# Query norms in a stage of their own, query products spread over the slots, outputs as triples: one change to a Perceiver layer on one core

## The reference

```
x = layernorm(x)
q = rmsnorm(x @ Wq, gq)                 # per head of 128 columns
k = rmsnorm(ctx @ Wk, gk);  v = ctx @ Wv
scores = q @ k.T / sqrt(128)            # 32 x 257 for each batch and head
out = softmax(scores) @ v
x1 = x + out @ Wo
```

## Time and profile before

| | |
|---|---|
| median of 3 runs | 2919.72 us (2918.31 to 2921.80) |
| profiled execution, own time | 2916.03 us |
| its span | 2914.2 us |
| mean granted TensorE clock | 0.944 |
| busy: PE, DVE, ACT, POOL | 2624.2, 2102.3, 1753.7, 1110.5 us |
| stages: keys; weights; attention's main block; the rest | to 770; 770 to 815; 815 to 2166; to 2914 us |

### The profile page before, as it was taken

One profiled execution on the slowest core, in us unless ns is written; L12 is line 12 of the kernel. 1 busy time (PEld: TensorE's weight loads), 2 busy tenths in 40 slices (PEclk: granted clock), 3 DMA queues, 4 the chain that ended last, 5 costly groups with the idle time before them and its releaser, 6 DMA issues. The chain is left out here.

```text
span 2914.2 us, 51949 instructions
## 1 busy us (share of the span) xinstructions
PE 2624.2 (90%) x14275; PEld 2095.6 (72%) x14275; DVE 2102.3 (72%) x4976; ACT 1753.7 (60%) x3450; POOL 1110.5 (38%) x1357
## 2 busy tenths in 40 slices
PE   8999999999779999999999999999968778847998
PEld 6777777777657888888888888888853434335887
DVE  7999999999556667766666677766644666667886
ACT  6777777777545566655556666655652433315776
POOL 0100010011024444544444444544425565634775
PEclk9999999999889999999999999999987878767999
DMA  1000000100222222222222222222220001020111
GB/s 45 25 24 24 24 24 26 31 24 25 91 58 67 65 84 84 82 65 73 69 68 72 73 84 84 73 70 68 69 71 22 22 22 44 15 80 30 55 51 39
DMA packets 191005, 154.56 MB, mean 53 GB/s; under 512 B 20658, under 2 KB 186899, under 8 KB 190227
## 3 DMA queue, kind: packets, MB, share of 16 engines
q1 hardware_dynamic: 190866, 153.14, 18.5%
HBM read 138.38 MB, written 14.69 MB: 53 GB/s over the span
## 5 line engine op out<-in xcount | busy, mean ns | idle before, releaser
L251 DVE TENSOR_REDUCE kn_ssq<-kn_sq 128x8 f32<-128x1024 f32 x514 | 620.6, 1215 | 71.7 <-ACT kn_sq L193 65.3
L193 ACT ACTIVATE kn_sq<-kn_keys 128x1024 f32<-128x1024 f32 x514 | 527.9, 1027 | 177.1 <-PE kn_keys L142 174.6
L748 ACT ACTIVATE ca_sc<-ca_sc,ca_low 128x257 f32<-128x257 f32 x512 | 254.4, 499 | 251.5 <-DVE ca_low L868 251.5
L930 POOL TENSOR_TENSOR ca_sc<-ca_sc,ca_rden 128x1028 f32<-128x1028 f32 x128 | 243.3, 1901 | 407.1 <-DVE ca_rden L850 407.1
L142 PE MATMUL kn_keys<-kn_wk_hi,kn_ct_hi 128*128 128x512 f32 x1028 | 334.5, 406 | 1.0 <-ACT kn_sq L193 1.0
L142 PE MATMUL kn_keys<-kn_wk_lo,kn_ct_hi 128*128 128x512 f32 x1028 | 319.9, 392 | 0.0
L142 PE MATMUL kn_keys<-kn_wk_hi,kn_ct_lo 128*128 128x512 f32 x1028 | 319.7, 392 | 0.0
L676 PE MATMUL ca_b_out<-ca_vo,ca_oT 128*128 128x256 f32 x1024 | 245.9, 383 | 2.9 <-ACT ca_oT L756 0.7
L823 DVE CUSTOM_DVE_ANT_0 ca_sc<-ca_b_sc,ca_rk,ca_rq_rows 128x257 f32<-128x257 f32 x512 | 229.9, 482 | 5.4 <-PE ca_b_last L657 3.7
L142 PEld LDWEIGHTS kn_keys<-kn_wk_lo,kn_ct_hi 128*128 128x128 f32 x1028 | 193.3, 188 | 44.5
L142 PEld LDWEIGHTS kn_keys<-kn_wk_hi,kn_ct_lo 128*128 128x128 f32 x1028 | 193.2, 188 | 43.4
(11 more groups left out here) (281 smaller groups left out, 6640.4 us busy)
## 6 DMA issues: line engine op xcount, KB each, us to landing
ca_rk<-key_norms SPq DMA_DIRECT2D x512, 128.5 KB, 2.9
kn_rows<-in_ctx_dram SPq DMA_DIRECT2D x128, 128.0 KB, 2.4
ca_rows<-in_ctx_dram SPq DMA_DIRECT2D x128, 128.0 KB
ca_xin<-in_x_dram SPq DMA_DIRECT2D x32, 128.0 KB, 2.7
ca_xres<-in_x_dram SPq DMA_DIRECT2D x32, 128.0 KB, 3.1
x_after_attention<-ca_x SPq DMA_DIRECT2D x32, 128.0 KB, 2.8
tm_xg<-x_after_attention SPq DMA_DIRECT2D x8, 512.0 KB, 4.6
tm_xr<-x_after_attention SPq DMA_DIRECT2D x8, 512.0 KB, 4.9
```

The costliest lines, as they stand in the source:

```text
L193: act.activation(sq[c][:, :], keys[c][:, :], ACT.Square).then_inc(sq_ready, 1)
L251: dve.tensor_reduce(ssq[s][:, t * H + c * (H // 2):t * H + (c + 1) * (H // 2)], sq[c][:, :].rearrange("p (h d) -> p h d", d=P), AX.X, ALU. ...
L748: act.activation(sc[n][:, g, :], sc[n][:, g, :], ACT.Exp, bias=low[n][:, g:g + 1], scale=1.0, accum_out=den[n][:, g:g + 1]).then_inc(exp_r ...
L930: pool.tensor_tensor(sc[m][:, :, :], sc[m][:, :, :], rden[m][:, :].unsqueeze(2).broadcast_to((P, 4, SKV)), ALU.mult)\
```

## The change

1. A new stage `query_norms` between `key_norms` and `cross_attention` normalises x, computes x Wq for all 32 tiles of 128 queries, and stores the transposed normalised x in parts (`xT`, 512 KB a superblock) and the inverse query norms (`rq`) in HBM. Wq is loaded and split by POOL during `key_norms`.
2. In `cross_attention` the phase of query products is gone. The first superblock's pairs of heads are made up front; those of the next superblock are made in the slots of the present one: none in slot 0, one in slots 1 to 6, two in slot 7. They use the bank `b_cols`, which `turn_ctx` uses too.
3. Outputs are triples: `oT` and `vo` are split (new DVE work `out_lo`).
4. The 257th key leaves `values`: its softmax weights are collected for four batches in 4 rows of `b_last`, stored, reloaded as a block-diagonal matrix and multiplied with the last keys' output rows (`last_values`, made up front), two matmuls a quad into `b_out`. The one-column casts go to POOL (`last_key`).
5. The program's loop is two superblocks long.

The core of the diff of `cross_attention`:

```diff
+        def pairs_ahead(b, bb):
+            if isinstance(b, int) and not 0 <= b < B - PER:
+                return ()
+            n = bb % PER
+            return (n - 1, n) if n == PER - 1 else (n - 1,) if n else ()
+        def pairs_before(b, bb):
+            n = b + PER - (bb % PER != 0)
+            return min(n, B) if isinstance(b, int) else n
...
         @block.tensor
...
+            def queries_ahead(b, bb, r, n):
...
+                pe.wait_ge(clo_ready, b + 2)
+                if n == PER - 1:
+                    pe.wait_ge(ulo_ready, b + PER)
+                queries(b_cols, n, xT[odd], odd)
             def turn_ctx(b, bb):
...
                 ge(pe, clo_ready, b)
+                ge(pe, ulo_ready, pairs_before(b - 1, bb - 1) if not isinstance(b, int) or b > 0 else 0)
...
-                    mm = pe.matmul(b_out[:, 0:DIM], oT[n][:, h, :], vo[:, h, :], start=(h == 0), stop=(h == H - 1))
+                    triple(b_out[:, 0:DIM], (oT_hi[n][:, h, :], oT_lo[n][:, h, :]), (vo_hi[:, h, :], vo_lo[:, h, :]), h == 0, False)
...
                 if live(b):
+                    scores(b, bb, 2)
+                    scores(b, bb, 3)
+                ahead = pairs_ahead(b, bb)
+                if ahead:
+                    queries_ahead(b, bb, r, ahead[0])
                 if live(b - 2):
                     values(b - 2, bb - 2)
+                if ahead[1:]:
+                    queries_ahead(b, bb, r, ahead[1])
...
         @block.scalar
...
                         act.activation(sc[n][:, g, :], sc[n][:, g, :], ACT.Exp, bias=low[n][:, g:g + 1], scale=1.0,
                                        accum_out=den[n][:, g:g + 1]).then_inc(exp_ready, 1)
+                ahead = pairs_ahead(b, bb)
+                if ahead:
+                    act.wait_ge(sc_ready, 4 * b + 4)
+                    queries(b_cols, 1 - bb // PER, ahead[0], b + PER)
                 if live(b - 2):
...
+                    act.activation(oT_hi[q][:, :, c * SQ:(c + 1) * SQ], b_val[:, :].rearrange("p (h q) -> p h q", q=SQ), ACT.Copy)\
+                        .then_inc(ohi_ready, 1)
+                if ahead[1:]:
+                    queries(b_cols, 1 - bb // PER, ahead[1], b + PER + 1)
...
         @block.vector
...
+            def slot(b, bb, r):
+                if live(b - 3):
+                    out_lo(b - 3, bb - 3, r)
...
                     dve.tensor_scalar(low[bb % 2][:, :], top[bb % 2][:, :], -1.0, None, ALU.mult).then_inc(low_ready, 1)
-                    split_last(b, bb)
...
+                for k, n in enumerate(pairs_ahead(b, bb)):
+                    queries(b_cols, 1 - bb // PER, n, b + PER + k)
...
         @block.sync
...
+                if bb % 4 == 2 and live(quad(bb, r) - 1, QUADS):
+                    Q = quad(bb, r) - 1
+                    n = (bb // 4 + 1) % 2
+                    store_stray(Q, n)
...
+                if bb % 4 == 3 and live(quad(bb, r) - 1, QUADS):
+                    load_stray(quad(bb, r) - 1, (bb // 4 + 1) % 2, 32 * (2 * r + (bb // 4 - 1) // 2 + 1))
```

More of the change, by code:

```diff
@@ L578, in triple, with queries @@
                 return pe.matmul(out, a_lo, w_hi, start=False, stop=final)
[L580 to L583 removed]
+            def queries(bank, n, x, odd):
+                for k in range(2):
+                    h = 2 * n + k
                     for a in range(2):
[L585 to L586 removed]
@@ L682, in slot @@
+                    pe.matmul(b_out[:, 0:DIM], ps_diag[n][:, :], vs_rows[n][:, 0, :], start=False, stop=False)
+                    pe.matmul(b_out[:, 0:DIM], ps_diag[n][0:64, :], vs_rows[n][0:64, 1, :], start=False, stop=True).then_inc(out_ready, 1)
+            def slot(b, bb, r):
+                Q = quad(bb - 6, r)
+                turn_p.r = r
                 if live(b + 1):
-                    turn_ctx.i = i
                     turn_ctx(b + 1, bb + 1)
                 if live(b - 2):
-                    turn_p(b - 2, bb - 2, i)
+                    turn_p(b - 2, bb - 2)
@@ L754, in slot @@
                     if c == 0:
-                        ge(act, out_ready, (b - 2) // 4 - 1 if isinstance(b, int) else 2 * i + (bb - 2) // 4 - 1)
-                    act.activation(oT[q][:, :, c * SQ:(c + 1) * SQ], b_val[:, :].rearrange("p (h q) -> p h q", q=SQ), ACT.Copy)\
-                        .then_inc(oT_ready, 1)
-            def body(i):
-                queries(i)
-                for bb in range(PER):
-                    slot(PER * i + bb, bb, i)
+                        ge(act, out_ready, quad(bb - 2, r) - 1)
@@ L808, in ctx_lo, with queries @@
+            def queries(bank, odd, n, done):
+                dve.wait_ge(uhi_ready, done)
+                dve.tensor_tensor(u_pair(u_lo, odd, n), bank[:, :].rearrange("p (h b q) -> p h b q", h=2, b=PER), u_pair(u_hi, odd, n).bitcast(F32),
+                                  ALU.subtract).then_inc(ulo_ready, 1)
             def ctx_lo(b, bb):
@@ L931, in slot @@
                         .then_inc(norm_ready, 1)
+                if live(b + 1):
+                    last_key(b + 1, bb + 1)
                 if live(b):
                     split_rows(b, bb)
-                if bb == 4 and i is not None and (not isinstance(i, int) or i + 1 < SBS):
-                    inverse_std(i + 1)
-            def body(i):
-                query_norms(i)
-                for bb in range(PER):
-                    slot(PER * i + bb, bb, i)
-            pool.wait_ge(const_ready, 8)
-            inverse_std(0)
-            run(pool, body, slot)
+            pool.wait_ge(stray_split, 2)
+            pool.wait_ge(const_ready, 4)
+            last_key(0, 0)
+            run(pool, slot)
 def time_mixing(nc, held, x1_dram, mu_dram, wx1_dram, wx2_dram, wr_dram, ww1_dram, ww2_dram, bw_dram, wk_dram, wv_dram,
```

652 lines of the change are left out of this document (367 added, 285 removed).

## The result

The changed kernel takes 3007.78 us (median of four runs, 3006.28 to 3009.52), the kernel before 2919.01 beside it: a ratio of 1.0304, interval 1.0286 to 1.0322. It is slower, as forecast, but by 89 us and not by 155; the time lies under the range's low end of 3020. The profiled execution has a span of 3007.7 us, 93.5 more than before.

What follows compares the result with a forecast made beforehand. Attention was taken as bound by the VectorE and ScalarE chain, with TensorE the limit in query products; 250 - 7.3 + 0 + 2 - 105 + 6 + 9 = +155; forecast 3074 us, range 3020 to 3140.

Steps and rivals of the forecast that it cites:

- break-even: Attention slots: the changed kernel is faster once a slot with a pair is under 7.8 us; forecast slot 9.28.
- the superblocks' term, -105: Attention loop: a superblock takes 75.5 us against 82.5, so 105 us less over 15.
- `turn_ctx` to `scaled` 2.59 less 0.31 = 2.28: End of a slot with a pair: 2.28 us from `turn_ctx` to the next `scaled`, three narrow transposes (0.31) gone.
- reciprocal to `scaled` 0.41: Slot without a pair: 0.41 us from VectorE's reciprocal to `scaled`, part of its 7.3 us.
- 0.84 leaves DVE's chain: Attention slots: the 257th key's `pl` and two casts leave VectorE's chain, 0.84 us, so `low` starts 3.43 after `scaled`.
- The clock: +9 forecast: Attention slots: TensorE's idle time lowers its clock in six slots, +9 us; bounds 0 and one for each of 105 slots.
- the rival of a fall in every slot: Attention slots: the clock falls in each slot with a pair, 99 more falls at 1.5 us, 3220; chance 7%.
- The new stage: +250: `query_norms`: a loop through POOL's power sets 7.2 us a tile over PE's 5.85, +250 us; bounds 208 and 265.
- POOL hides: New stage: POOL's power does not pace it (cheaper, or ACT's squares get ahead), 42 us less, 3032; chance 12%.
- The sum of the head: Head of attention: query load, eight pairs and last keys' products take 38.9 us instead of 36.9, +2.
- DVE and ACT alone pace them: Attention slots: PE's transposes are early, slots take 8.2 us, 113 less, 2961; chance 5%.
- PE's work paces: Attention slots: `u_lo` does not hold `turn_ctx`, slots take PE's 7.68 us, 208 less, 2866; chance 8%.

Runs made afterwards that it cites:

- Experiment 1: Changed kernel with the query pairs behind the values and in the banks of the scores instead of `b_cols`: 2848.72 us, ratio 0.9766.
- experiment 2: Changed kernel with TensorE doing the values before the first query pair, same bank and same wait: 3008.25 us, ratio 1.0310.
- experiment 4: Changed kernel with outputs as plain fp32 products again, without `out_lo`: 3010.53 us, ratio 1.0311.
- Experiment 8: One more VectorE instruction per slot on the changed kernel: 3078.88 us; attention loop written out on the changed kernel: 2983.41 us, on the kernel before: 2905.94 us.
- Experiment 3: Changed kernel with GpSimd's inverse root taken one tile later in the new stage: 2976.41 us, ratio 1.0195.
- experiment 9, first run: Changed kernel with pairs in the banks of the scores, inverse roots one tile later and plain fp32 outputs: 2804.71 us, ratio 0.9618.
- second run: Changed kernel with pairs in the scores' banks, inverse roots one tile later, plain fp32 outputs and the attention loop written out: 2792.43 us, ratio 0.9571.

## Why the prediction came out as it did

*Direction: right, and shown.* The new stage costs more than the superblocks give back, and the pair in a shared bank is why they give so little. Experiment 1 takes away only that wait (experiment 2 excludes the order) and the kernel crosses to the other side. The prediction's break-even was a slot of 7.8 us; at 7.40 the kernel is faster than the one before, at 8.9 slower.

*The step that failed: the superblocks' term, -105, measured -141.* By its own parts: a slot without a pair was 6.80 and not 7.3; six with one summed to 53.7 (1308.17 to 1361.90) and not 55.7; the one with two was 12.1 (1437.31 to 1449.44) and not 12.5. That is 2.9 us a superblock, 43 in fifteen; the stops at the loop's end gave 10 of it back. The mechanism was right; three pieces of the chain were mis-sized. For a slot with one pair the first and the third below, 0.19 and 0.13, make the difference: 9.28 - 0.32 = 8.96, and 53.7 / 6 = 8.96 (single slots took 8.84 to 9.18). In all three, an end of the interval had been set by something other than what would set it in the new chain. For the first two, PE's rows of the slot before and of the slot after:

```profile
1109.55 0.40 PE L669 MATMUL ca_b_val<-ca_pl,ca_last 65*128 65x512 f32 x1
...
1109.79 0.38 PE L629 MATMUL ca_b_cols<-ca_ident,ca_rows 128*128 128x128 f32 x2
...
1111.56 0.28 PE L578 MATMUL ca_b_sc<-ca_cT_hi,ca_u_lo 128*128 128x258 f32 x1
```

```profile
1332.95 0.44 PE L850 MATMUL ca_b_cols<-ca_ident,ca_rows 128*128 128x128 f32 x2 [1.27 <-DVE ca_u_lo L1000]
...
1334.45 0.28 PE L825 MATMUL ca_b_sc<-ca_cT_hi,ca_u_lo 128*128 128x258 f32 x1
```

- "`turn_ctx` to `scaled` 2.59 less 0.31 = 2.28" began at the start of a weight load (1109.56) that lay 0.23 us ahead of its matmul (1109.79), because PE was still at the last value product. Behind an idle PE load and matmul start together (1332.95), and the interval is 2.09 (to 1335.04). The other end hid nothing: the last product of score group 0 starts 0.59 ahead of `scaled` in both slots.
- "reciprocal to `scaled` 0.41", taken for the slots without a pair, was most likely a wait for PE as well: in that slot of before `scaled` came 0.59 behind the last product of its score group, just as in the slot after, where DVE's wait ends with PE's scores. With PE early, `scaled` follows by 0.09 behind `oT_lo` and the reciprocal (2188.71 to 2188.80), and by 0.18 in experiment 4, where the reciprocal comes out of an idle stretch. Other slots of before had 0.34; what sets those was not taken apart.
- "0.84 leaves DVE's chain" counted from the start of `pl`; with the gap ahead of it 0.97 left (`low` at +4.27 before, +3.30 after). Experiment 8 puts a like instruction back at 0.56.

Only the third was sized by a run; the first two are read from the traces.

*The clock: +9 forecast, some 2 us found.* I had taken the falls of the first superblock for six more slots. Busy time by stretch in the changed kernel's first superblock, then over one of its later slots with a pair and behind the first jump at the loop's end:

```profile
1091.00:1097.00 6.00, 3.55 (x18) 3.25 (x18) 3.02 (x16) 3.12 (x12) 3.98 (x7) 0.67 0.84 222
1097.00:1103.00 6.00, 5.48 (x23) 4.88 (x23) 2.51 (x11) 1.47 (x3) 3.97 (x7) 0.50 0.25 57
1103.00:1106.00 3.00, 2.73 (x13) 2.73 (x14) 1.21 (x8) 1.72 (x7) 0.00 (x0) 0.50 0.22 65
```

```profile
1317.11:1326.11 9.00, 7.27 (x55) 6.44 (x54) 4.95 (x21) 4.30 (x14) 4.21 (x8) 1.00 0.29 83
1374.00:1376.00 2.00, 2.00 (x12) 1.92 (x11) 0.77 (x2) 1.01 (x2) 0.72 (x1) 0.50 0.45 131
```

The clock fell during the first of these stretches, in which PE was busy 3.55 of six microseconds, and stayed at 1.2 GHz (0.50) until about 1107. The first three slots took 9.08, 9.01 and 9.20 us and the fourth 8.74, so the fall cost about 1 us at most. (By reciprocals the second slot looks 3.4 us too long, 12.12, but 3.5 of it is the wait for PE ahead of its `scaled`, and the interval ahead of it is 5.73. In the kernel before, too, the reciprocals that I took the earlier trace rows begin behind the stretch with the low clock; the slot that holds it goes from `scaled` at 869.32 to 878.02 and took 8.70, 1.7 more than the others.) Later slots idle PE 1.7 us each and stay at 1.00. The clock falls again behind two of the five jumps at the loop's end, at the first behind a stop of PE of 2.9 us, and once in the last superblock, at 2248. The superblocks with those two jumps took 75.4 and 74.8 us, the three with the others 74.3 to 74.5. Together that is some 2 us, an estimate from these times. The rule of the Trainium skill (TensorE: Matmul & The Clock Gate, HAM oscillation — how this bites in real kernels) that bursts of matmuls with waits between them start cold again was the rival of a fall in every slot; the trace bears it out in these few places, and not in the other slots, some hundred.

*The new stage: +250, measured +242.* The loop through POOL is right in every member; a tile was 6.93 us and not 7.2, because my 0.3 us of gaps were not there, and that is the 8 us. Experiment 3 shows the loop, and that the rival "POOL hides" (42 us less) was one reordering away: it gave 31. The power's price, 158 ns a column, held to 1%.

*The head, the drain.* Stores of `last_values` land in a median of 2.1 us, and I had taken 2.8; the last superblock's slots were 6.8 to 7.1 and not 7.3. With the drain it is 9.7 us, read from the trace alone; no run took it apart. The sum of the head was also added up wrong: 5 + 11.4 + 2 + 17 + 3 is 38.4 and not 38.9. The Wq split under the key stage cost 1.0, the weight stage gave 6.8 of 7.3.

*The rivals.* "DVE and ACT alone pace them" had the right engines, once the bank was free: 7.40 instead of 8.2. "PE's work paces" had the right side for that kernel and the wrong mechanism. The range failed because its low end stood on one rival (POOL hides), while three pieces of the slots were mis-sized, all to the same side, and counted fifteen superblocks long; most of the other terms erred to that side too, so little cancelled.

## What to carry to other kernels

When the producer is early, look for who frees the buffer last: the pair's products were done 1.5 us before anyone wanted them, and the bank they sat in cost more than the new stage's pacing did. Place a filler product in a bank whose next user is late in the order of its engine, not first. And before an interval is carried from one chain to another, read what began and what ended it: if an end was set by another engine, or is a weight load that starts while its engine is still busy, the interval holds slack. Measure slots of two kernels from the same event, one that lies behind the wait.

## What the runs showed of the hardware

The jump back at the end of a loop body is not free. Rows of the changed kernel, of DVE and of PE, at one of its five:

```profile
1374.42 0.69 DVE L1028 TENSOR_TENSOR ca_oT_lo<-ca_b_val,ca_oT_hi 128x512 fp32r<-128x512 f32 x1 [2.62 <-issue]
```

```profile
1373.15 0.29 PEld L850 LDWEIGHTS ca_b_cols<-ca_ident,ca_rows 128*128 128x128 f32 x2 [2.90 <-issue]
```

Neither had anything to wait for that the profile shows. In straight code (experiment 8) the stops are gone. A superblock with a jump took 1.7 to 2.8 us more than its neighbours. In the kernel before, the jumps come just ahead of the block of query products, where DVE had a wait of its own for ACT (2.79 us), and cost about 0.5 us each (experiment 8). Slots inside a loop were also 0.1 to 0.2 us longer than the same slots in straight code (8.61 against 8.41, 8.94 against 8.74), in the kernels where a PE wait closes the slot; with the bank free and plain outputs it was the other way, 61.0 us a superblock inside the loop (experiment 9, first run) against 61.1 to 61.2 written out (second run). What in the loop form costs this was not taken apart.
